# Two expert layers of a four-layer network: how token rows reach their buffer, and when the router sees them

## The reference

```python
router_logits = x @ Wr                                   # 256 -> 8
router_probs = softmax(router_logits)
expert_idx = argmax(router_probs)
out = p_max * (gelu(x @ W1[e] + b1[e]) @ W2[e] + b2[e])   # e = expert_idx, F = 1024
x = x + tanh(g_ffn[0]) * out
```

## Time and profile before

| | us |
|---|---|
| median of 3 runs (lowest, highest) | 3350.38 (3349.03, 3354.73) |
| the profiled execution, its own time | 3352.86 |
| its span, first to last instruction | 3351.1 |
| TensorE busy | 2880.7 (86%) |
| VectorE busy | 1918.6 (57%) |
| ScalarE busy | 1409.0 (42%) |
| GpSimd busy | 598.1 (18%) |

### The profile page before, as it was taken

One profiled execution on the slowest core, in us unless ns is written; L12 is line 12 of the kernel. 1 busy time (PEld: TensorE's weight loads), 2 busy tenths in 40 slices (PEclk: granted clock), 3 DMA queues, 4 the chain that ended last, 5 costly groups with the idle time before them and its releaser, 6 DMA issues. The chain is left out here.

```text
span 3351.1 us, 46532 instructions
## 1 busy us (share of the span) xinstructions
PE 2880.7 (86%) x13948; PEld 2113.6 (63%) x13949; DVE 1918.6 (57%) x3700; ACT 1409.0 (42%) x2923; POOL 598.1 (18%) x544
## 2 busy tenths in 40 slices
PE   5695789965997989999599999999999997256997
PEld 4684455535885779999366666666666664234664
DVE  4314465405555354444688888888888884442332
ACT  1233534421211224445277676777767775100000
POOL 0122101111331200000201111111111111154554
PEclk9797879986998879999799999999999998587998
DMA  1342000003232010000011000001100000425776
GB/s 39 128 136 82 14 14 14 14 0 110 82 99 88 1 39 26 25 13 1 23 27 24 22 18 19 20 16 29 21 22 20 16 15 3 184 81 160 168 170 136
DMA packets 157228, 177.45 MB, mean 53 GB/s; under 512 B 37664, under 2 KB 130998, under 8 KB 155510
## 3 DMA queue, kind: packets, MB, share of 16 engines
q1 hardware_dynamic: 120150, 116.15, 12.1%
q0 software_dynamic: 20512, 35.54, 4.7%
q10 hardware_dynamic: 16416, 24.12, 2.1%
HBM read 105.77 MB, written 49.18 MB: 46 GB/s over the span
## 5 line engine op out<-in xcount | busy, mean ns | idle before, releaser
L2065 DVE TENSOR_TENSOR l3a_pt_lo<-l3a_pt,l3a_pt_hi 128x512 fp32r<-128x512 f32 (+2 forms) x640 | 463.8, 730 | 96.4 <-ACT l3a_pt L1959 92.1
L1958 ACT ACTIVATE l3a_pt_hi<-l3a_banks 128x512 fp32r<-128x512 f32 (+2 forms) x640 | 382.5, 598 | 322.7 <-PE l3a_banks L1904 258.8
L1959 ACT ACTIVATE l3a_pt<-l3a_banks 128x512 f32<-128x512 f32 (+2 forms) x640 | 378.0, 591 | 0.0
L2039 DVE TENSOR_REDUCE l3a_maxima<-l3a_banks 128x1 f32<-128x1178 f32 x256 | 351.1, 1375 | 1.8 <-PE l3a_banks L1855 0.6
L1904 PE MATMUL l3a_banks<-l3a_pt_hi,l3a_v 128*65 128x512 f32 (+2 forms) x640 | 286.6, 448 | 8.0 <-ACT l3a_out L1973 8.0
L1914 PE MATMUL l3a_banks<-l3a_q,l3a_k 128*128 128x512 f32 (+2 forms) x640 | 257.1, 402 | 7.4 <-DVE l3a_q L2002 4.6
L1915 PE MATMUL l3a_banks<-l3a_q,l3a_k 72*128 72x512 f32 (+5 forms) x640 | 253.8, 397 | 0.0
L1904 PE MATMUL l3a_banks<-l3a_pt_hi,l3a_v_lo 128*65 128x512 f32 (+2 forms) x640 | 252.7, 395 | 0.0
L1904 PE MATMUL l3a_banks<-l3a_pt_lo,l3a_v 128*65 128x512 f32 (+2 forms) x640 | 252.5, 394 | 0.0
L1855 PE MATMUL l3a_banks<-l3a_k,l3a_q 128*128 128x512 f32 (+1 forms) x768 | 213.1, 387 | 18.6 <-DVE l3a_maxima L2039 17.5
L1855 PEld LDWEIGHTS l3a_banks<-l3a_k,l3a_q 128*128 128x128 f32 x768 | 139.6, 192 | 64.0 <-DVE l3a_maxima L2039 41.9
(11 more groups left out here) (563 smaller groups left out, 6065.0 us busy)
## 6 DMA issues: line engine op xcount, KB each, us to landing
l3f_w<-in_L_ffn_w SPq DMA_DIRECT2D x96, 256.0 KB, 3.1
l0f_w<-in_L_ffn_W ACTq DMA_DIRECT2D x12, 1024.0 KB, 6.5
l3f_slots_x<-l3f_empty SPq DMA_DIRECT2D x10, 1168.0 KB, 15.4
l3f_x_rows<-l3f_slots_x SPq DMA_DIRECT2D x32, 292.0 KB, 3.9
l1f_w<-in_L_ffn_W ACTq DMA_DIRECT2D x18, 512.0 KB, 5.2
l2f_w<-in_L_ffn_w SPq DMA_DIRECT2D x16, 512.0 KB, 4.5
l3a_q<-l3a_q SPq DMA_DIRECT2D x64, 128.0 KB, 2.3
l3a_k<-l3a_k SPq DMA_DIRECT2D x64, 128.0 KB, 2.3
```

Source lines behind the costliest of these rows:

```text
L1958: act.activation(a.pt_hi[0:rows, n % a.pt_slots, :], a.st_bank[0:rows, n % 2, :], ACT.Exp, bias=bias, scale=scale)
L1959: act.activation(a.pt[0:rows, n % 4, :], a.st_bank[0:rows, n % 2, :], ACT.Exp, bias=bias, scale=scale).then_inc(a.exped, 1)
L2039: dve.tensor_reduce(a.maxima[:, n:n + 1], banks.rearrange("p a b -> p (a b)")[:, 0:KEYS], AX.X, ALU.max).then_inc(a.maxed, 1)
L2065: dve.tensor_tensor(a.pt_lo[0:rows, slot, :], a.pt[0:rows, n % 4, :], a.pt_hi[0:rows, slot, :].bitcast(F32), ALU.subtract).then_inc(a.lo_m ...
```

## The change

In both layers three things change.

1. **Rows come through a second buffer.** Gathers land in `x_land`, and GpSimd copies `x_land` to `x_tile` when the tile before has been turned (`move_tile`). GpSimd also makes `in_index` and `out_index`, which VectorE made. TensorE's `turn_rows` waits for that copy (`x_ready`) where it waited for the gather. The first two gathers go out back to back, since `table` has both. The wait for a scatter's landing moves behind the next gather.
2. **Raw rows are turned and routed at once.** `turn_raw_and_route` turns `chip.x` itself, before it is normalised, and makes the logits of tile n - 3 behind the turning of tile n.
3. **Logits are centred later.** Since the rows are raw, logits become `(raw - mean * column sum of Wr) * inv_std`. The column sums are two matmuls with a matrix of ones; VectorE makes `offset` before it normalises, and two steps on the logits are new. The bias rows' transpose and its copy move behind the routing.

```diff
+ROUTE_BEHIND = 3
+def turn_raw_and_route(pe, chip, s, psum, p_logits, p_sums, w, experts, loaded, routed, summed):
+    for n in range(TILES + ROUTE_BEHIND):
+        if n < TILES:
+            if n >= TURN_BANKS:
+                pe.wait_ge(s.turned_read, n + 1 - TURN_BANKS)
+            for c in range(DC):
+                ins = pe.transpose(psum[:, n % TURN_BANKS, c * P:(c + 1) * P], chip.x[:, n, c * P:(c + 1) * P], chip.ident[:])
+            ins.then_inc(s.turned, 1)
+        if n == ROUTE_BEHIND:
+            pe.wait_ge(*loaded)
+            for c in range(DC):
+                ins = pe.matmul(p_sums, chip.ones[:], w[:, c, :], start=c == 0, stop=c == DC - 1)
+            ins.then_inc(summed, 1)
+        if n >= ROUTE_BEHIND:
+            t = n - ROUTE_BEHIND
+            pe.wait_ge(s.turned_read, t + 1)
+            for c in range(DC):
+                ins = pe.matmul(p_logits[:, t * experts:(t + 1) * experts], chip.xt[:, c, t * P:(t + 1) * P], w[:, c, :],
+                                start=c == 0, stop=c == DC - 1)
+    ins.then_inc(routed, 1)
+def centred_logits(dve, step, chip, logits, p_logits, offset):
+    experts = logits.shape[2]
+    step(dve.tensor_tensor(logits, p_logits, offset, ALU.subtract))
+    step(dve.tensor_tensor(logits, logits, spread(chip.inv_std[:], experts), ALU.mult))
...
         @block.gpsimd
...
-            pool.indirect_dma_start(x_tile[:], None, rows, bass.IndirectOffsetOnAxis(table[:, 0:1], 0)).then_inc(x_loaded, 16)
-            pool.wait_ge(indexed, 1)
-            pool.indirect_dma_start(x_tile[:], None, rows, bass.IndirectOffsetOnAxis(in_index[:], 0)).then_inc(x_loaded, 16)
+            pool.indirect_dma_start(x_tile[:], None, rows, bass.IndirectOffsetOnAxis(table[:, 0:1], 0)).then_inc(first_loaded, 16)
+            pool.indirect_dma_start(x_land[:], None, rows, bass.IndirectOffsetOnAxis(table[:, 1:2], 0)).then_inc(x_loaded, 16)
             pool.wait_ge(placed, 1)
...
-                pool.wait_ge(indexed, at + 1)
+            def move_tile(at, first):
+                pool.wait_ge(x_loaded, at * 16)
                 pool.sem_inc(taken, 1)
-                pool.indirect_dma_start(x_tile[:], None, rows, bass.IndirectOffsetOnAxis(in_index[:], 0)).then_inc(x_loaded, 16)
+                pool.tensor_copy(in_index[:], column(table, at + 1)).then_inc(indexed, 1)
+                pool.wait_ge(x_turned, at)
+                pool.sem_inc(taken, 1)
+                pool.tensor_copy(x_tile[:], x_land[:]).then_inc(x_ready, 1)
+                pool.wait_ge(indexed, at)
+                pool.wait_ge(x_ready, at)
+                pool.sem_inc(taken, 1)
+                pool.indirect_dma_start(x_land[:], None, rows, bass.IndirectOffsetOnAxis(in_index[:], 0)).then_inc(x_loaded, 16)
+                if not first:
+                    pool.wait_ge(y_stored, at * 16 - 16)
+                    pool.sem_inc(y_free, 1)
+                pool.tensor_copy(out_index[:], column(table, at - 1)).then_inc(out_indexed, 1)
                 pool.wait_ge(y_kept, at + 1)
+                pool.wait_ge(out_indexed, at)
                 pool.sem_inc(taken, 1)
                 pool.indirect_dma_start(sums, bass.IndirectOffsetOnAxis(out_index[:], 0), y_tile[:], None).then_inc(y_stored, 16)
-                pool.wait_ge(y_stored, at * 16)
-                pool.sem_inc(y_free, 1)
...
         @block.tensor
-                        turn_rows(at * 16 + 16)
+                        turn_rows(x_ready, at)
...
         @block.vector
             row_statistics(dve, chip, norm_steps, 0, chip.x)
+            step = Steps(dve, route_steps)
+            dve.wait_ge(summed, 1)
+            mean_offsets(dve, step, chip, offset[:], p_y[:, 448:448 + E])
             normalize_dve(dve, chip, turn, chip.x)
-            dve.wait_ge(b1_turned, 1)
-            dve.tensor_copy(b1[:], p_y[:, 0:E * FC]).then_inc(b1_kept, 1)
             dve.wait_ge(routed, 1)
...
-                dve.tensor_copy(in_index[:], column(table, turnings)).then_inc(indexed, 1)
...
-                    dve.tensor_copy(out_index[:], column(table, at - 1))
```

More of the change, by code:

```diff
@@ L650, in _ @@
         def _(pe):
+            turn_raw_and_route(pe, chip, turn, p_hidden, p_route[:, 0:TILES * E], p_y[:, 448:448 + E], wr, E, (loaded, 16), routed, summed)
+            pe.wait_ge(route_steps, 1)
             pe.wait_ge(b_loaded, 16)
             pe.transpose(p_y[:, 0:E * FC], b1_rows[:], chip.ident[0:E * FC, 0:E * FC]).then_inc(b1_turned, 1)
[L653 to L660, removed]
             pe.wait_ge(chose, 1)
@@ L666, in _, with turn_rows @@
             pe.sem_inc(y_done, 1)
-            def turn_rows(loads):
-                pe.wait_ge(x_loaded, loads)
+            def turn_rows(landed, count):
+                pe.wait_ge(landed, count)
                 for c in range(DC):
@@ L881, in _ @@
+            pool.indirect_dma_start(x_land[:], None, rows, bass.IndirectOffsetOnAxis(in_table[:, 1:2], 0)).then_inc(x_loaded, 16)
             pool.wait_ge(placed, 1)
-            count = pool.value_load(all_tiles[0:1, 0:1], min_val=1, max_val=MAX_TILES)
-            g = one_register(pool, "l1f_pool_g")
-            with pool.Fori(0, count):
-                at = pool.snap(g, min_val=1, max_val=MAX_TILES)
-                pool.wait_ge(indexed, at + 1)
-                pool.sem_inc(taken, 1)
-                pool.indirect_dma_start(x_tile[:], None, rows, bass.IndirectOffsetOnAxis(in_index[:], 0)).then_inc(x_loaded, 16)
+            later = pool.value_load(later_tiles[0:1, 0:1], min_val=1, max_val=MAX_TILES)
@@ new lines, in move_tile @@
+            def move_tile(at, first):
+                pool.wait_ge(x_loaded, at * 16)
+                pool.sem_inc(taken, 1)
+                pool.tensor_copy(in_index[:], column(in_table, at + 1)).then_inc(indexed, 1)
+                pool.wait_ge(x_turned, at)
+                pool.sem_inc(taken, 1)
+                pool.tensor_copy(x_tile[:], x_land[:]).then_inc(x_ready, 1)
+                pool.wait_ge(indexed, at)
+                pool.wait_ge(x_ready, at)
+                pool.sem_inc(taken, 1)
+                pool.indirect_dma_start(x_land[:], None, rows, bass.IndirectOffsetOnAxis(in_index[:], 0)).then_inc(x_loaded, 16)
+                if not first:
+                    pool.wait_ge(y_stored, at * 16 - 16)
+                    pool.sem_inc(y_free, 1)
+                pool.tensor_copy(out_index[:], column(out_table, at - 1)).then_inc(out_indexed, 1)
@@ L894, in _ @@
+            with pool.Fori(0, later):
+                move_tile(pool.snap(g, min_val=2, max_val=MAX_TILES), False)
                 pool.reg_add(g, g, 1)
-            done = pool.snap(g, min_val=1, max_val=MAX_TILES + 1)
-            pool.wait_ge(x_loaded, done * 16 + 16)
+            done = pool.snap(g, min_val=2, max_val=MAX_TILES + 1)
+            pool.wait_ge(x_loaded, done * 16)
+            pool.wait_ge(y_stored, done * 16 - 16)
             pool.sem_inc(all_stored, 1)
@@ L1031, in _ @@
             expert_bases(dve, step, chip.ones, rank[:], upto[:], compare[:], thresholds[:], tiles[:], ends[:], tile_counts[:])
-            step(dve.tensor_tensor(all_tiles[:], ends[:, E - 1:E], tiles[:, E - 1:E], ALU.add))
+            step(dve.scalar_tensor_tensor(later_tiles[:], ends[:, E - 1:E], -1.0, tiles[:, E - 1:E], ALU.add, ALU.add))
             for k in range(K):
@@ L1054, in keep_turned @@
                 dve.tensor_copy(xt_tile[:], p_xt[:, 0:D]).then_inc(x_kept, 1)
-                dve.tensor_copy(in_index[:], column(in_table, turnings)).then_inc(indexed, 1)
             keep_turned(1)
```

90 lines of the change are left out of this document (48 added, 42 removed).

## The result

The changed kernel takes 3326.7 us (median of 4 runs, 3323.1 to 3328.8) where before takes 3349.7 (median of 4). The ratio is **0.993**, 95% interval 0.9912 to 0.9948: 23 us less, between 17 and 29.

The account below looks back on a forecast made before the run. The prediction took routing to end with TensorE's logits and the loops to be bound by TensorE. Routing -5.8, late tiles +0.9, stalls -6.7 and last tiles -0.3 sum to -11.9: 3350.4 becomes 3338.5 us, range 3330 to 3355.

Parts of the forecast that it names:

- p: Expert loops: GpSimd's time from the scatter's end to the end of the row copy, taken at 0.90, between 0.37 and 1.39.
- the gap inside p: Expert loops: GpSimd's idle time between a scatter and the copy behind it, taken at 0.40; 0 to 0.54 thought possible.
- the price of a record: Routing: TensorE's time per transpose or matmul record, taken at 0.22 us at clock 0.50; 92 records take 20.2 us.
- the ends: Last tile of each layer: the out_index copy, 0.13, is won ahead of the last scatter; -0.3 us in all.
- the two copies: Expert loops, on GpSimd: in_index taken at 0.13 us and the 256-column row copy at 0.37 us.
- late steady tiles: Expert loops: layer 0's steady tiles 0.06 late each, +0.9 us; layer 1's in time.
- the twelve stalls: Expert loops: TensorE's waits for gathers, 11.3 us together; 0.56 of 0.87 won in the slow case, -6.7 us in all.
- the low end: Expert loops: p at 0.37, where no steady tile is late and all 11.3 us of waits are won.
- GpSimd becomes the bound: Rival for the loops: copy 0.72, gap 0.54, p 1.39, steady tiles late; +15.5 us, 3366; chance 0.12.
- The limit from which a steady tile is late: Expert loops: the row copy is in time for TensorE's turning with p up to 0.84 in layer 0, 0.92 in layer 1.
- the two more steps: Routing: VectorE's two added steps on the logits cost 0.65 us a layer, 1.3 in all.
- full clock: Rival for the routing: clock 1.00, 0.114 us a record, normalising decides; wins 21.0 instead of 5.8 us, 3323; chance 0.10.

Follow-up runs that it names:

- x1: The kernel before with only the new loops (second buffer, copy on GpSimd, moved wait), routing as before: 0.9968 of before, -10.7 us.
- x3: The kernel before with only GpSimd's wait for a scatter's landing moved behind the next gather; one buffer, no copy: 0.9973 of before, -9.1 us.
- x5: The changed kernel with x_land and x_tile 1280 columns wide, so GpSimd's copy moves 1280 columns instead of 256: 1.0003 of before.
- x2: The kernel before with only the new routing (raw rows routed at once, logits centred later), loops as before: 0.9963 of before, -12.4 us.
- x0: The changed kernel run once more, nothing altered, on the chip of its two halves: 0.9931 of before, -23.1 us.
- x6: The changed kernel with each logit matmul 128 columns wide instead of 8: 0.9903 of before, -32 us.
- x8: New routing with 128-column logit matmuls, ROUTE_BEHIND 6, separate semaphore for layer 1's router weights; one-buffer loop with only the wait moved: 0.9892 of before, -36 us.
- x9: The kernel before with each logit matmul 128 columns wide instead of 8: 0.9992 of before.
- x10: The changed kernel with x_land and x_tile 640 columns wide, so GpSimd's copy moves 640 columns instead of 256: 0.9943 of before.

## Why the prediction was half right

Two terms of the sum were mis-sized, both to the same side: the gap inside p, taken at 0.40 and measured at nil, and the price of a record in the routing, taken at 0.22 and measured at 0.20. With the two put right, and layer 1's late bias counted, the prediction's own sum is -11.6 for the loops and -8.6 for the routing, some -20 in place of -11.9; the measured -23 has that inside its interval.

**The loop: the mechanism right, one term mis-sized.** Forecast -6.1 with the ends, measured -10.7 (x1). The step that failed is p. Of its three pieces the two copies were right within 0.04; the gap, 0.40, does not exist. The prediction had named that case ("it can be 0 if the queue runs ahead") and not taken it. A p of 0.53 changes both terms that hang on it: the 0.9 us of late steady tiles is 0, and of the twelve stalls not 0.56 but all 0.87 each are won, which is the low end that the prediction named ("all 11.3 at the low end"). With p = 0.53 its own formula gives -11.3 and -0.3, within the interval of x1. The gap was read from the wrong kind of pair: a scatter that follows a gather, and the loop's end, not a copy that follows a scatter.

**The stalls' cause: right.** The prediction said that what helps is that the gather no longer stands behind the scatter's landing. x3 shows that this alone gives the gain. It did not say the consequence, that the second buffer and GpSimd's copy are then not needed.

**The rival "GpSimd becomes the bound": right in kind.** It did not happen in the changed kernel; x5 made it happen. At p = 1.38 (0.12 + 1.26, x5) the loop's gain is gone and the routing's too. The limit from which a steady tile is late is p = 0.94, not 0.84; at 0.53 the kernel is 0.4 us away from it.

**The ends.** Behind the last scatter nothing was forecast (the -0.3 is the `out_index` copy ahead of it), and the one pair of traces has -0.9 and -1.0 there. Of this, 0.3 a layer is the time from the last scatter's start to the fetch of the outputs on SP (2.82 and 2.84 before, 2.52 and 2.53 after). x3, where VectorE still makes `out_index`, has 2.48 and 2.52, so it comes with the moved wait and not with that copy. As for the rest: from the last scatter to the next stage's first transfer, layer 0 takes 14.8 to 15.1 us in the three traces with the old loop and 14.1 to 14.2 in the ten with a new one; layer 1 takes 35.0 to 36.1 and 34.6 to 35.9, which do not separate. What lies behind the fetch was not looked into.

**The routing: clock right, one term mis-sized.** Forecast -5.8, measured -12.4 (x2, -16.8 to -8.0). The clock was at 0.50, layer 0's weights came when forecast (layer 1's bias, 3.3 us into the stage and not 2.5, took back 0.8), and the two more steps cost 0.6 a layer. The step that failed is the price of a record: 0.22 was taken from the logit records alone, and one of the mixed order takes 0.20, so the 92 records took 18.5 us in place of 20.2, 1.7 a layer. That makes it -8.6, and the pair of profiles has -4.2 - 5.7 + 1.1 = -8.7. The base does not explain what is left. It was one profile, and over three traces with the old routing (before, x1, x3) it took 24.3, 26.8 and 24.0 us in layer 0 and 27.5, 25.2 and 24.8 in layer 1: together 50.9 on average, less than the 51.8 of before's profile, while the new one takes 41.7 to 41.9 (after, x0, x2). By these rows the saving is 50.9 - 41.8 - 1.1 = 8.0 us of the 12.4; the rest is open. It may be no more than the interval's width.

**The rival "full clock"** named 3323, nearer to the measured 3327 than the forecast, and yet its mechanism did not happen: the clock was at 0.50. A time alone would have confirmed the wrong story. x6 then made it happen, and in layer 0 its limit was the one that the rival named, the end of the normalising (in layer 1 it was so in x8). On the rule of the Trainium skill that the prediction weighed against the rows (TensorE: Matmul & The Clock Gate, Part 1, "activity releases the throttle"): read as "busy", the trace contradicts it, with 18.47 of 18.50 us busy at 0.50; in x6 and x9 the same engine, as busy in the same stages, ran at 1.00 through logit matmuls of 128 columns.

**The untouched stages** account for 1.9 of the 24.0 us between the two traces; the attention between the layers took 454.1 us in before's profile and 450.3 to 453.0 in the twelve others. That is noise of single profiles, and the reason why the halves were timed and not only read.

## What to carry to other kernels

When a queue serves two streams, look first at what each wait in it stands ahead of: moving one wait behind the next independent transfer gave here all that could be measured of what the second buffer gave, with no copy. The gap between two instructions differed here with the pair (0.30 from a gather to a scatter, nil from a scatter to a copy); for a pair that no row shows, take both ends, and see which terms of the sum hang on it. A stage that runs at the lower clock, though the engine is busy, may gain by wider matmuls: the same logits in matmuls of 128 columns instead of 8 took 0.106 us a record instead of 0.20. By the rows that was worth 10.9 us on top of the new order (41.8 to 30.9) and 4.7 without it (50.9 to 46.2), where VectorE's normalising still stood ahead of the logits; the time bears out the first (x6, -32 against -23) and does not show the second (x9).

## What the runs showed of the hardware

- In the changed kernel TensorE's granted clock was at 0.50 through 18.5 us of unbroken work in which most matmuls had 8 columns; in x6, with 128 columns in their place, it rose to 1.00 in the same stage and stayed. Sixteen times the columns made a record faster, 0.106 instead of 0.20 us.
- GpSimd starts a copy in the instant in which the scatter ahead of it ends (201.26), but the transfer that waits for its own copy starts 0.79 after the copy's end (201.79 to 202.58).
- GpSimd's copies took longer beside VectorE's long additions with two inputs. At the first tile of layer 1, the two copies take 1.02 and 1.40 us instead of 0.20 and 0.40:

```profile
799.57 3.69 DVE L1124 TENSOR_TENSOR chip_x<-chip_x,l1f_gbf 128x1024 f32<-128x1024 f32 x3
799.80 1.02 POOL L939 COPY l1f_in_index<-l1f_in_table 128x1 int32<-128x1 int32 x1 [1.90 <-issue]
...
800.78 1.40 POOL L942 COPY l1f_x_tile<-l1f_x_land 128x256 f32<-128x256 f32 x1
```

The Trainium skill (GPSIMD Engine Reference, section "Specifications") says that the two engines share their interfaces to SBUF and lists operations of VectorE with two SBUF inputs as a cause of contention; this row agrees. At the first tile of layer 0, without such additions, the copies take 0.19 and 0.39. The loss at the copy of the rows does not grow with its width: 1.40 for 0.40, 1.72 for 0.72 (x10), 2.25 for 1.25 (x5), each time 1.0 us, as of an operation that waits and not of one that runs slower. No run took VectorE's additions away.
